# Local attention: order of projection, squares, rotation and sums in the four steps that fill the pipeline

## The reference, cut to what matters

```python
for l in range(DEPTH):
    h = shift_token(x)
    q, k, v = jnp.split(h @ wqkv, 3, axis=-1)       # 256 -> 3 x 512
    q = l2norm(q) * qs
    k = l2norm(k) * ksc
    q, k = rotary_xpos(q, k)                         # cos and sin per row
    o = local_attention(q, k, v)                     # own window and the one before, masked softmax
    x = x + o @ wo
    x = x + gated_mlp(layernorm(shift_token(x)))
```

## Time and profile before

| | us |
|---|---|
| median of 3 runs | 4276.4 |
| lowest and highest of them | 4274.67, 4279.17 |
| the profiled execution, its own time | 4274.23 |
| its span | 4272.5 |
| first layer's local attention, first instruction | 843.58 |
| second layer's local attention, first instruction | 1492.70 |

### The profile page before, as it was taken

One profiled execution on the slowest core, in us unless ns is written; L12 is line 12 of the kernel. 1 busy time (PEld: TensorE's weight loads), 2 busy tenths in 40 slices (PEclk: granted clock), 3 DMA queues, 4 the chain that ended last, 5 costly groups with the idle time before them and its releaser, 6 DMA issues. The chain is left out here.

```text
span 4272.5 us, 94807 instructions
## 1 busy us (share of the span) xinstructions
PE 3799.4 (89%) x38248; PEld 2138.6 (50%) x38248; DVE 3377.6 (79%) x5459; ACT 2555.2 (60%) x3426; POOL 1298.5 (30%) x1092
## 2 busy tenths in 40 slices
PE   7999999679988969988986899999999999866996
PEld 4888888535554535554553332232333333434664
DVE  5788888779987569987887999999998978584444
ACT  5566666545553336553343777787888887644553
POOL 2123231277864267864340000000000000033552
PEclk8999999889999989999997999999999999977998
DMA  4011110133332033331072000000000000034664
GB/s 102 13 32 34 37 32 19 46 72 62 66 47 53 15 73 63 62 54 33 15 172 36 9 9 1 9 2 2 9 2 1 9 2 9 4 100 94 122 129 112
DMA packets 378678, 188.50 MB, mean 44 GB/s; under 512 B 291796, under 2 KB 369320, under 8 KB 377768
## 3 DMA queue, kind: packets, MB, share of 16 engines
q1 hardware_dynamic: 355656, 147.00, 16.3%
q0 software_dynamic: 13440, 21.24, 2.8%
q10 hardware_dynamic: 9184, 14.68, 1.3%
HBM read 78.33 MB, written 38.58 MB: 27 GB/s over the span
## 5 line engine op out<-in xcount | busy, mean ns | idle before, releaser
L2380 DVE TENSOR_REDUCE s_tops<-ps 128x2 f32<-128x1024 f32 (+3 forms) x1152 | 1250.8, 1131 | 139.8 <-PE ps L2266 100.9
L2349 ACT ACTIVATE s_weights<-ps 128x1024 f32<-128x1024 f32 (+3 forms) x1152 | 1093.7, 953 | 340.6 <-PE ps L2279 191.1
L2301 PE MATMUL ps<-s_weights,v_flat 128*32 128x256 f32 (+1 forms) x8704 | 690.6, 389 | 7.5 <-ACT s_o_t L2355 6.1
L2260 PE MATMUL ps<-keys,s_q 48*128 48x512 f16 (+3 forms) x2304 | 433.5, 374 | 47.1 <-DVE s_tops L2380 27.1
L2279 PE MATMUL ps<-s_q,keys 50*128 50x512 f16 (+3 forms) x2304 | 433.2, 373 | 45.8 <-DVE s_tops L2380 33.6
L2416 POOL CAST s_shift<-s_minus_top 128x16 f16<-128x16 f32 x32 | 6.3, 198 | 1426.5 <-DVE s_minus_top L2387 1426.5
L653 PE MATMUL ps<-a_qt,a_kt 128*128 128x256 f16 x3072 | 375.3, 273 | 3.9 <-POOL s_ones L608 3.9
L2279 PEld LDWEIGHTS ps<-s_q,keys 50*128 50x128 f16 x2304 | 112.0, 93 | 509.6 <-issue 252.1
L1246 PE MATMUL ps<-attention_w,la_yt 128*128 128x512 f16 x1152 | 292.2, 402 | 37.5 <-DMA la_yt<-la_y_parts 30.1
L653 PEld LDWEIGHTS ps<-a_qt,a_kt 128*128 128x128 f16 x3072 | 300.9, 98 | 40.3 <-POOL s_ones L608 4.1
L1321 ACT ACTIVATE la_weights<-ps 128x1024 f32<-128x1024 f32 x124 | 127.0, 1024 | 302.3 <-PE ps L1236 302.3
(11 more groups left out here) (387 smaller groups left out, 7239.5 us busy)
## 6 DMA issues: line engine op xcount, KB each, us to landing
ex_whole<-in_L_ffn_w_dram ACTq DMA_DIRECT2D x14, 1024.0 KB
qk_parts<-a_parts SPq DMA_DIRECT2D x64, 128.0 KB, 4.0
keys<-qk_parts SPq DMA_DIRECT2D x48, 128.0 KB, 5.3
s_q<-qk_parts SPq DMA_DIRECT2D x48, 128.0 KB, 4.9
x<-in_x_dram SPq DMA_DIRECT2D x8, 512.0 KB, 9.0
attention_w<-attention_split SPq DMA_DIRECT2D x2, 2048.0 KB, 9.1
la_table<-in_rotary_dram SPq DMA_DIRECT2D x64, 64.0 KB, 2.1
a_table<-in_rope_dram POOLq DMA_DIRECT2D x8, 512.0 KB, 5.7
```

Source lines behind the costliest of these rows:

```text
L2260: mm = pe.matmul(m.ps[:, bank, 0:width], b.q[rows(half, KEY_PARTS * L1_DH), place % 2, pair, t * P:(t + 1) * P], m.keys[rows(half, KEY_PAR ...
L2301: mm = pe.matmul(m.ps[h * QUAD:(h + 1) * QUAD, OUT, begin:end], m.v_flat[:, first:first + QUAD], weights[:, a % 2, h, begin:end], start=(k ...
L2349: act.activation(weights[:, a % 2, 2 * pair:2 * pair + 2, skip:CHUNK], m.ps[:, bank:end + 1, skip:CHUNK], ACT.Exp).then_inc(s["exp"], 1)
L2380: dve.tensor_reduce(tops[:, u % 2, :, i % 2, t, c], m.ps[:, bank:end + 1, 0:width], AX.X, ALU.max).then_inc(s["max"], 1)
```

## The change

In steps below 0 the work on tile i + 4 is put first: on TensorE `project_q` and `project_k` ahead of both `find`s, on ScalarE `square` ahead of `high`, on VectorE `rotate` and `sums` ahead of the `find`s and of `low`. On GpSimd step -4 (`FILL`) makes the tables of tiles 0 and 1, and each of the steps -3 to -1 makes the table of the next tile at its end, behind `norms`; step 0 then makes none, and from step 1 on the order is the old one. `norms(w)` gets a wait for `normalise(w - 1)`, which stands ahead of it on the same engine. Steps from 0 on are otherwise untouched.

```diff
+        FILL = -4
+
...
                 def norms(w):
                     pool.wait_ge(s["ss"], w + 1)
+                    after(pool, s["qk"], w)
...
                     if exists(i + 3):
                         normalise(i + 3)
-                    if exists(i + 4):
+                    if i == FILL:
+                        tables(0)
+                        tables(1)
+                    if i > 0 and exists(i + 4):
                         tables(i + 4)
...
                         add(i + 4)
                         norms(i + 4)
+                    if FILL < i < 0:
+                        tables(i + 5)
...
                 def step(i):
+                    if i < 0 and exists(i + 4):
+                        project_q(i + 4)
+                        project_k(i + 4)
                     if exists(i + 2):
                         find(i + 2, 0)
-                    if exists(i + 4):
+                    if i >= 0 and exists(i + 4):
                         project_q(i + 4)
...
-                    if exists(i + 4):
+                    if i >= 0 and exists(i + 4):
                         project_k(i + 4)
...
+                    if i < 0 and exists(i + 4):
+                        square(i + 4)
                     if exists(i + 3):
                         high(i + 3)
-                    if exists(i + 4):
+                    if i >= 0 and exists(i + 4):
                         square(i + 4)
...
                 def step(i):
+                    if i < 0 and exists(i + 4):
+                        rotate(i + 4)
+                        sums(i + 4)
                     if exists(i + 2):
                         find(i + 2, 0)
...
-                    if exists(i + 4):
+                    if i >= 0 and exists(i + 4):
                         rotate(i + 4)
                     if exists(i):
                         divide(i, 0)
-                    if exists(i + 4):
+                    if i >= 0 and exists(i + 4):
                         sums(i + 4)
```

## The result

| us | before | after |
|---|---|---|
| median of 20 runs | 4270.92 | 4280.89 |
| lowest and highest | 4264.52, 4287.62 | 4270.39, 4287.39 |
| the profiled execution, its own time | 4274.23 | 4282.38 |
| its span | 4272.5 | 4280.6 |
| first instruction of the first layer's local attention | 843.58 | 843.79 |

The medians differ by 10.0 us. The ratio over all the runs is 1.002, with a 95% interval of 1.0012 to 1.0027: 8.5 us slower on 4270.9, between 5.1 and 11.5. The forecast was 7.2 slower, at 4283.6. The medians now rest on 20 runs each; the three from which the prediction took its level (4276.4) lay 5.5 high.

What follows compares the result with a forecast made beforehand. In the fill no engine is full; a loop across engines, 12.29 us a turn, sets the pace. `low(2)` 3.6 later in each of two layers, 7.2 on 4276.4, gives 4283.6; own range 4279 to 4286, overall 4276 to 4289.

Steps and rivals of the forecast that it cites:

- The sum of 3.6 a layer: First layer's fill, added up from `rotate(0)` at 853.86: `low(2)` ends at 894.4, 3.6 us later than before.
- (a): Fill: whether GpSimd's `norms(1)`, due at 867.77, is held by VectorE's `low(0)`, running until 868.9; between 0 and 1.1 us.
- (b): TensorE's projection bursts in the fill: 5.26 us each; with two short bursts the layer's loss would be 1.2.
- (d): New wait of `norms` on GpSimd: at most 0.12 us late on 31 tiles, taken as 0.
- (e): `square` ahead of `high` on ScalarE delays `high(2)` to 886.5, long before `low(2)` is asked for: 0.
- The handshake: Fill: VectorE's `find` follows `sums`, TensorE's `find` waits for it; tile 3's projections start at 878.0, banks free at 874.3.
- signs of being wrong: In the trace of after: `find(2, 0)` early, a steady step of changed length, or a fill clock near 1.
- The gain gets through: Rival: step 0 follows `rotate(3)`, so each layer wins 6.3 us, 4263.8 in all; chance 0.05.
- The clock comes up: Rival: TensorE at 2.4 GHz in all the fill's bursts, GpSimd sets the pace; no change, 4276.4; chance 0.14.
- Held by `normalise(3)`: Rival: GpSimd's `normalise(3)` gets in before `low(2)`, which ends 5.4 or 6.5 us late: 4287.2 to 4289.4; chance 0.16.
- Given back later: Rival: TensorE's later gaps, 0.84 us a step, take up the delay; near 4277; chance 0.05.

Runs made afterwards that it cites:

- the frame: Program cut after the first layer's local attention, that stage run eight times: order before 4439.51, changed 4470.01 us; with the MLP's weight loads last, 4422.43 and 4448.58.
- low-early order: Changed kernel with both `find`s and `low(2)` ahead of `rotate(3)`, and `low(1)` ahead of `sums(2)`: 4268.60 us, ratio 0.9997; in the frame, loads last, 4407.99.
- The filler: Changed kernel of the frame, loads last, with eight more matmuls of 512 columns behind `project_k` in each step below 0: 4442.35 us.
- the repeated trace of after: The changed kernel run again, unaltered, for a second trace: 4278.48 us, ratio 1.0017 to the kernel before.

## Why the prediction was right

**What is handed on is `low(2)`, not `rotate(3)`: right, and shown.** In all kernels of the frame the mean of `high(31)` moves with the mean start of `low(2)` to within 0.6 us, and in the low-early order `rotate(3)` is late and the stage is short.

**The sum of 3.6 a layer: right in its path, and half a microsecond too large at the place where it was taken.** From the stage's first instruction the end of `low(2)` is 3.2 and 3.4 later in the first trace, 3.6 and 3.3 in the second, and only 2.9 and 2.5 in the means of the two pairs of the frame. Counted from `rotate(0)`, as the sum counts, the frame has 3.1. Yet the medians of the frame say 3.8 and 3.3 a stage, since behind `low(2)` another 0.8 is lost until `high(31)`, where the text expected all that follows to be shifted by as much. The traces show it in the step from `high(3)` to `high(4)`. Where the first projection behind step 1's `find` (six matmuls) runs fast, in 1.47, the step takes 12.3; where it runs at the low level, in 2.35 to 2.74, the step takes 13.3 to 13.8. The low level is there in 13 of the frame's 16 stages of the changed order, and in 2 of the 16 of before (four more of before lie between, 1.96 to 2.01, with steps of 12.5 to 12.7). So behind the changed fill TensorE was more often at the lower clock in step 1, a term that the sum lacks; why it was is open. The forecast of 7.2 for both layers thus comes as near as it does in part by luck: one term half a microsecond too large, another left out.

The forecast's stations of the first layer were `rotate(3)` 884.4 and `low(2)` ending at 894.4; the trace has 884.40 and 893.04 + 1.21 = 894.25, from a stage that began 0.21 later. That they agree to this is luck too: two terms cancelled, as the text had left open.
- (a) The hold of norms by `low(0)` came: 3.82 against 2.92, 0.9 of the 1.1, and `rotate(2)` then waited for the tables (872.75; the sum had 871.8 without the hold and 872.9 with it). By the Trainium skill, page "SBUF — State Buffer", section "SBUF: two separate sides", a VectorE operation with two SBUF inputs, such as `low`, and a GpSimd operation that reads SBUF share a pair of ports, and whichever starts first holds it to its end. The trace agrees: `low(0)` started first (867.84, 868.00), and it was norms that was long.
- (b) The bursts of tiles 1 and 3 took 5.28 and 4.47 against 5.26 each in the sum: 0.8 back.
- (d) The new wait of norms: a steady step is as long as before (12.29 to 12.30). (e) showed no cost; `high(2)` ran from 884.26 to 885.30, where the text had 886.5.

**GpSimd's part** had no cost of its own in the forecast. Alone, in the old order, it costs 0.7 to 0.8 a stage (`low(2)`, `high(31)`). In the changed kernel the sum had it in its place, since tile 2's tables stand there behind norms.

**The handshake: right as a cause, and shown** by moving it: with the `find`s ahead of the bound, all else kept, `high(31)` is 1.3 earlier than in the order of before instead of 3.3 later.

**The signs.** `rotate` of tiles 1, 2 and 3 came 3.3, 5.9 and 6.6 nearer to the stage's first instruction; the text announced 4, 6 to 7 and 5 to 6, though its own sum gives 3.4, 6.7 and 6.4. Tile 3's projection started as TensorE's second `find` ended (878.84; 878.51 + 0.39) and 3.7 after `rotate(2)` ended, and VectorE's `find(1, 0)` (889.18) stood right behind L1442. `low(2)` and `find(2, 0)` came 3.2 and 3.3 later, inside the announced 3 to 5. None of the signs of being wrong came.

**The rivals.** *The gain gets through* is out: `find(2, 0)` is late. *The clock comes up* didn't happen (0.65). The filler brought its condition about only in part: the projections of tiles 1 and 2 were fast, tile 3's was not, in spite of the added matmuls; a gap of 4.52 lies ahead of it. So its price of no change is not tested in full. `rotate(2)` came 17.6 after `rotate(0)` where the rival has 16.9 (870.8 - 853.86), because `low(0)` waited out `add` and then held norms: 0.7 that the rival lacks. Faster bursts gave 0.5 of the 3.6, or 1.0 counted from `rotate(0)` (39.1 against 40.1). *Held by `normalise(3)`* was decided by a hundredth of a microsecond: `low(2)` 893.04, `normalise` 893.05. It had a chance of 0.16 and would have cost 1.8 more a layer. The sum, with 893.2 for both, could not tell; but it isn't chance from one run to the next. In all 28 stages of the changed order that were traced (four in the whole program, 24 in the frame, the filler among them) `low(2)` started 0.01 or 0.02 ahead of `normalise(3)`, which then took 2.95 or 2.96 instead of 1.90. Both engines come to it from nearly the same instant, the ends of `add(3)` and `sums(3)` (889.24 and 889.27 here), and what lies between took the same time in each stage. *Given back later* looked true in the first layer of the first trace, and isn't. There the step with the loads took 15.5 us before and 13.0 in after. Kernel before, the timeline behind that step's wait:

```profile
949.06 0.39 PE L1214 MATMUL ps<-la_kt,la_qt 64*128 64x256 f16 x4 [2.33 <-DMA la_qt<-la_parts]
949.38 1.90 PE L1246 MATMUL ps<-attention_w,la_yt 128*128 128x512 f16 x6
951.08 1.06 PE L1232 MATMUL ps<-band,spread 128*128 128x256 bf16 x4
952.07 1.46 PE L1236 MATMUL ps<-la_qt,la_kt 64*128 64x256 f16 x12
```

and the same in after:

```profile
951.79 0.39 PE L1222 MATMUL ps<-la_kt,la_qt 64*128 64x256 f16 x4 [1.46 <-DMA la_qt<-la_parts]
952.12 1.47 PE L1254 MATMUL ps<-attention_w,la_yt 128*128 128x512 f16 x6
953.42 0.60 PE L1240 MATMUL ps<-band,spread 128*128 128x256 bf16 x4
953.95 0.83 PE L1244 MATMUL ps<-la_qt,la_kt 64*128 64x256 f16 x12
```

TensorE waited 2.33 for the transposes and went on at a lower clock, here 1.46 and stayed fast. In the second layers it was the other way round (15.3 and 16.0), the repeated trace of after has 13.4 and 13.6, and in the frame the means agree to 0.3. So three of the four stages of the changed kernel in the whole program happened to have a short step there; in the frame, with eight stages of each order, both spread over the same range. What remains is 3.3 to 3.8 a stage, 6.6 to 7.6 in all, inside the measured 5.1 to 11.5. That the fill makes the whole of the 8.5 is argued from this agreement; the whole program's traces don't show it.

**The level** was the weakest number: 4283.6 stood on a median of three and lies 2.7 above the 4280.89 of after, while the difference alone was missed by 1.3 (7.2 against 8.5), or by 2.8 if the two medians are subtracted.

## What to carry over

When work is pulled ahead in the fill of a pipeline, look for what the first full step's in-order lists ask for last; an operation that starts 6 us sooner is worth nothing, or less, if the one that is asked for now stands behind it. A small back-and-forth between two engines belongs into the shadow of a longer operation of a third, ahead of the instruction that would wait that operation out. An effect of some microseconds in one stage is measured by repeating the stage; the whole program's trace has accidents as large in stages that nobody touched.

## What the runs showed of the hardware that was not expected

- The same first projection of a stage took between 4.0 and 5.3 us from one stage to the next of the same program, and moved everything behind it by as much; counted from the `rotate` behind it, the rest of the old order's fill repeats to 0.03 us in 18 stages.
- The low clock of the fill reached into the first full steps (six matmuls in 2.35 to 2.74 instead of 1.47) in 13 of 16 stages of the changed order, and made one step of 12.3 a step of 13.3 to 13.8.
- Ten weight loads, issued ahead of small transposes on the same queue, lengthen one step of 12.3 to anything between 12.9 and 16.9 from one stage to the next of the same program.
